# Token choice by one-hot matmuls: the one-hot tile and its values laid out with the contracted columns innermost

## The reference, cut to what matters

```
logits = x @ gate_w.T                      # 4096 tokens x 16 experts
scores = softmax(logits, axis=-1)
for each expert e: the 512 tokens with the highest score[:, e] are chosen
out   += score * (gelu(x Wg) * (x Wu)) Wd  # of the chosen tokens alone
out   += shared expert of all tokens
```

## Time and profile before

| what | us |
|---|---|
| median of three runs | 4539.38 |
| profiled execution, its own time | 4539.38 |
| span of its trace | 4537.7 |
| TensorE matmul busy | 3656.6 (81%) |
| VectorE busy | 2486.8 (55%) |
| ScalarE busy | 1439.2 (32%) |
| GpSimd busy | 1668.4 (37%) |
| from the first `hot` comparison to the copy of `slots` | 3699.21 to 3761.30 |

### The profile page before, as it was taken

One profiled execution on the slowest core, in us unless ns is written; L12 is line 12 of the kernel. 1 busy time (PEld: TensorE's weight loads), 2 busy tenths in 40 slices (PEclk: granted clock), 3 DMA queues, 4 the chain that ended last, 5 costly groups with the idle time before them and its releaser, 6 DMA issues. The chain is left out here.

```text
span 4537.7 us, 53885 instructions
## 1 busy us (share of the span) xinstructions
PE 3656.6 (81%) x17474; PEld 1672.2 (37%) x17563; DVE 2486.8 (55%) x3976; ACT 1439.2 (32%) x2018; POOL 1668.4 (37%) x1362
## 2 busy tenths in 40 slices
PE   8889999979997899977596504057797998999994
PEld 3322222223332433325354302023355554555553
DVE  5589999945552155533523497955695572111113
ACT  2247777743332233332132302011253221111111
POOL 0032222226665056662263073723552221222221
PEclk9979999989998999988698756578898998999997
DMA  5542323211102511113224402023354013333333
GB/s 174 186 74 60 73 62 69 56 58 35 38 26 73 193 37 38 40 41 116 91 85 137 168 17 93 0 84 92 114 155 151 28 38 109 105 97 92 103 82 83
DMA packets 323883, 382.97 MB, mean 84 GB/s; under 512 B 52016, under 2 KB 252992, under 8 KB 322688
## 3 DMA queue, kind: packets, MB, share of 16 engines
q1 hardware_dynamic: 270912, 285.83, 20.4%
q0 software_dynamic: 35776, 73.97, 6.4%
q10 hardware_dynamic: 17024, 20.97, 1.3%
HBM read 240.69 MB, written 135.76 MB: 83 GB/s over the span
## 5 line engine op out<-in xcount | busy, mean ns | idle before, releaser
L571 DVE TENSOR_REDUCE modulated_mx<-modulated_ring 128x1 f32<-128x512 f32 x1024 | 651.5, 683 | 52.2 <-PE modulated_ring L478 46.0
L555 ACT ACTIVATE modulated_probs<-modulated_scores 128x1024 f32<-128x1024 f32 x512 | 496.1, 1021 | 182.0 <-PE modulated_scores L499 181.9
L2861 DVE TENSOR_TENSOR expert_h<-expert_gelu,expert_bank 128x512 f32<-128x512 f32 x128 | 88.0, 688 | 391.6 <-PE expert_bank L2829 391.6
L2789 POOL DMA_INDIRECT scratch_acc<-expert_y,expert_idx x64 | 101.0, 1579 | 485.0 <-DVE expert_y L2866 442.9
L508 PE MATMUL modulated_acc<-modulated_probs,modulated_v 128*32 128x512 f32 x2048 | 273.5, 606 | 0.6 <-ACT modulated_probs L555 0.6
L478 PE MATMUL modulated_ring<-modulated_k,modulated_q 64*128 64x512 bf16 x1024 | 239.5, 399 | 34.1 <-DMA modulated_v<-scratch_v 23.0
L499 PE MATMUL modulated_scores<-modulated_q,modulated_k 128*128 128x512 bf16 x945 | 255.7, 383 | 10.9 <-issue 5.1
L910 POOL TENSOR_TENSOR causal_total<-causal_total,causal_probs 128x1024 f32<-128x1024 f32 x96 | 225.6, 2350 | 86.5 <-ACT causal_probs L831 85.5
L910 POOL TENSOR_TENSOR meta_total<-meta_total,meta_probs 128x1024 f32<-128x1024 f32 x96 | 225.6, 2350 | 86.5 <-ACT meta_probs L831 85.5
L2829 PE MATMUL expert_bank<-expert_xT,expert_wg 128*128 128x512 f32 x512 | 243.2, 598 | 7.8 <-ACT expert_xT L2841 7.8
L853 DVE TENSOR_REDUCE causal_mx<-causal_maxima 128x2 f32<-128x1024 f32 x120 | 146.0, 1217 | 183.8 <-PE causal_maxima L737 183.8
(11 more groups left out here) (471 smaller groups left out, 6970.1 us busy)
## 6 DMA issues: line engine op xcount, KB each, us to landing
expert_wg<-x_WgT SPq DMA_DIRECT2D x16, 1024.0 KB, 4.9
expert_wu<-x_WuT SPq DMA_DIRECT2D x16, 1024.0 KB, 6.9
expert_wd<-x_WdT SPq DMA_DIRECT2D x16, 1024.0 KB, 5.4
modulated_k<-scratch_k_part SPq DMA_DIRECT2D x192, 64.0 KB, 3.0
modulated_q<-scratch_q_part SPq DMA_DIRECT2D x192, 64.0 KB, 3.1
scratch_v<-proj_v SPq DMA_DIRECT2D x8, 1024.0 KB, 6.7
modulated_v<-scratch_v SPq DMA_DIRECT2D x16, 512.0 KB, 4.6
scratch_M<-steps_snap SPq DMA_DIRECT2D x16, 512.0 KB, 3.3
```

The source lines that it names most:

```text
L555: nc.scalar.activation(probs[u % NPROBS][i][:], sc[i][:], ACT.Exp, scale=SCALE).then_inc(s_exp, 1)
L571: V.tensor_reduce(mx[h % 2][:, x // 2, 1 - j % 2, j // 2, x % 2:x % 2 + 1], ring[bank_of["max", 4 * m + j]][:], AX.X, ALU.max).then_inc(s_ ...
L2789: added[j].done(G.indirect_dma_start(out=scr["acc"], out_offset=bass.IndirectOffsetOnAxis(ap=idx[j][a][:], axis=0), in_=y[j][:, a, :], in_ ...
```

## The change: layout of the one-hot tile and of the values

The shapes are turned round; the computation and the results are the same.

```
-        B_ = st.sb("values", [P, CT * VALS, NT, NE], BF16)
+        B_ = st.sb("values", [P, NT, NE, CT * VALS], BF16)
...
-        cols, low = st.sb("cols", [P, P, NE], BF16), full("low", BF16)
-        hot = [st.sb(f"hot{j}", [P, P, NE], BF16) for j in range(2)]
+        cols = st.sb("cols", [P, P])
+        hot = [st.sb(f"hot{j}", [P, NE, P], BF16) for j in range(2)]
...
-            G.iota(cols[:], pattern=[[1, P], [0, NE]], ...)
+            G.iota(cols[:], pattern=[[1, P]], ...)
...
-  last = nc.tensor.matmul(slots[:, e, :], hot[t % 2][:, :, e], B_[:, :, t, e], ...)
+  last = nc.tensor.matmul(slots[:, e, :], hot[t % 2][:, e, :], B_[:, t, e, :], ...)
...
-            step(V.tensor_single_scalar(low[:], lo[:], 1.0, ALU.subtract))
+            step(V.tensor_single_scalar(lo[:], lo[:], 1.0, ALU.subtract))
...
-                step(tt(B_[:, a * VALS], where[a][:], tile_no[:], ALU.mult))
-                step(V.tensor_scalar(B_[:, a * VALS + 1], where[a][:], tok_no[:], None, ALU.mult))
+                step(tt(B_[:, :, :, a * VALS], where[a][:], tile_no[:], ALU.mult))
+                step(V.tensor_scalar(B_[:, :, :, a * VALS + 1], where[a][:], tok_no[:], None, ALU.mult))
                 for c in range(3):
-                    step(tt(B_[:, a * VALS + 2 + c], where[a][:], part[c][:], ALU.mult))
+                    step(tt(B_[:, :, :, a * VALS + 2 + c], where[a][:], part[c][:], ALU.mult))
...
-                tt(hot[t % 2][:], cols[:], low[:, t:t + 1, :].broadcast_to([P, P, NE]), ALU.is_equal).then_inc(s_hot, 1)
+                tt(hot[t % 2][:], cols[:].unsqueeze(1).broadcast_to([P, NE, P]), lo[:, t, :].unsqueeze(2).broadcast_to([P, NE, P]),
+                   ALU.is_equal).then_inc(s_hot, 1)
```

More of the change, by code:

```diff
@@ L2521, in _ @@
             G.affine_select(out=below[:], in_=below[:], compare_op=ALU.is_gt, fill=0.0, base=0, pattern=[[1, P]], channel_multiplier=-1).then_inc(s_made, 1)
-            G.iota(cols[:], pattern=[[1, P], [0, NE]], base=0, channel_multiplier=0, allow_small_or_imprecise_dtypes=True).then_inc(s_made, 1)
+            G.iota(cols[:], pattern=[[1, P]], base=0, channel_multiplier=0, allow_small_or_imprecise_dtypes=True).then_inc(s_made, 1)
             G.iota(tile_no[:], pattern=[[1, NT], [0, NE]], base=0, channel_multiplier=0, allow_small_or_imprecise_dtypes=True).then_inc(s_made, 1)
@@ L2612, in _ @@
                 for e in range(NE):
-                    last = nc.tensor.matmul(slots[:, e, :], hot[t % 2][:, :, e], B_[:, :, t, e], start=(t == 0 and e == 0), stop=(t == NT - 1),
+                    last = nc.tensor.matmul(slots[:, e, :], hot[t % 2][:, e, :], B_[:, t, e, :], start=(t == 0 and e == 0), stop=(t == NT - 1),
                                             skip_group_check=True)
```

## The result

The changed kernel has a median of 4597.33 us over five runs (4588.27 to 4600.99), the kernel before one of 4542.89 over five: a ratio of 1.0122, 95% interval 1.0106 to 1.0138. That is 54 us slower. The forecast was 4562.5, with a range up to 4574: the sign was right, the size wrong, and the measured time lies outside the range.

A forecast was written before the change was run, and what follows sets the result against it. TensorE bounds the stretch up to tile 23, then both engines alternate; after the change VectorE does. Values 3.5, GpSimd 1.3 and 8.7, comparisons 70.5 and last tile 1.28 us give +23.2, forecast 4562.5 us, range 4549 to 4574.

The forecast's parts named there:

- the price of the values' writing: Ahead of the first comparison: products with `part` at 692 ns, `tok_no` ones at 426, 3.5 us more in all.
- the sum: Values' extra 3.5 us, GpSimd's 1.3 and 8.7, comparisons 70.5, last tile 1.28: copy of `slots` 23.2 us later.
- The comparison: The 32 one-hot comparisons on VectorE: starts 2.20 us apart instead of 1.14, 70.5 us of work against 36.6.
- GpSimd beside VectorE: GpSimd's `h` and `y` hold up a gapless VectorE: 1.3 us ahead of the comparisons, 8.7 beside them.
- my bound of 0.2 us: TensorE's loads and matmuls: only the last tile's 1.28 us counts, left as it is; bound 0 to -0.2.
- the first rival: TensorE's clock falls in the first part, a pair takes 6.1 us: 13 us more, 4576; chance 0.08.
- GpSimd does not cut in: Rival: comparisons hold their place and GpSimd waits, contention falls to today's or less: +13 to +17, 4554; chance 0.12.
- not slower: Rival: the comparison keeps more of its pace, under 1.90 us between starts TensorE hides it for 24 tiles; 4537; chance 0.06.

The follow-up runs named there:

- The added products: Kernel before, with 512-element products of various output and input steps added at the stage's end: bfloat16 outputs 730, 1295, 2424 ns at 4, 8, 16 bytes.
- the one-hot tile alone: Kernel before, with only the lines of `cols`, `low` and `hot` changed to the new layout: 4562.75 us, ratio 1.0046.

## Why the prediction was wrong

One row of the kernel before bears on the step that failed, a copy by ScalarE in another stage (min/median/max ns):

```profile
L1838 ACT ACTIVATE mproj_laid<-mproj_bank x16: 1005/1044/1073, 2577.9 to 2805.6; 128x512 f32<-128x512 f32 x16
```

- *The step that failed* is the price of the values' writing: "With an output that steps over 20 elements I take 692: 12 x 0.266 = 3.2 us; the bounds are 0 and 3.2", with "The products with `tile_no` stay" and an upper bound of 692 for `tok_no`. I looked for what a step does to the pace of the inputs (packed or not) and closed the range there, at the price of a dense output. The text says itself that "no row shows a stepped output alone"; the bound from above was then no bound. And one row did show it. ScalarE writes L1838 in the kernel before to every 16th float32 element and takes 1044 ns for 512, where its dense copies of 512 take 597 (L2554). That row, shown above, gives no 2399 ns, but it shows that a stepped output has a price of its own. Measured: 2399 ns for all sixteen two-input products and 1370 for the four others, and the stretch at 49.0 us against the 20.4 of the sum (15.6 + 3.5 + 1.3). The comparisons' stretch came out 2.3 us under the sum (78.2 against 80.5), so the two stretches missed by 26.3. The medians missed by 31.2 (54.4 against 23.2); the other 4.9 lie outside the stretches or in the spread between executions. The Trainium skill has the line that I did not weigh: "Advanced Engine Details and Errata", section "SBUF Cachelines", has lines of 16 bytes and a penalty where every access goes to another line. The added products agree with the 16 bytes, and in two-input products half-written words cost more than twice as much as the line alone.
- *The comparison* was right: 2279 ns, starts 2.20 us apart, from the nearest row by shape and repetition. That the one-hot tile alone landed on 4562.75 is in part chance, as said with that run.
- *GpSimd beside VectorE* was right in kind. Beside the comparisons it was 6.5 us (32 times 2481 less 2279, mean and median), not 8.7: all four `y` of the chunk before fell into the longer writing of the values, none on the comparisons. In the values' stretch I had added 1.3 us; it fell instead, from 3.9 to some 2.7.
- *TensorE* gained more than my bound of 0.2 us: the stage's end after the last comparison is 0.7 us, not 1.28. What I drew from the Trainium skill's "TensorE: Matmul & The Clock Gate", section "Weight-path perf modes — Fast Weight Load (FWL) and DoubleRow" (no gain from packed weights) goes further than the section does: it names packed and strided reads for the fast load, and that both are equally fast was my inference. The rows show otherwise: in the median, packed weights take 96 to 113 ns a load here, strided ones 167 to 168.
- *The clock* fell as the first rival says, to a mean of 0.77 in the first part, where I had said that under 0.9 would prove me wrong. It cost next to nothing: VectorE waited 0.3 us in all. A job at half speed takes 3.76 us, but two tiles only some 1.1, a pair 4.9 us, about what VectorE needs with GpSimd's share (4.4 and up to 1.3), and some jobs ran at full speed. The rival's price had all jobs at half speed and used the old 2.33.
- *GpSimd does not cut in* and *not slower* are out: 3.06 us for an `h` shows it waiting for a comparison, and then the next comparison waiting for it; and the comparisons start 2.20 us apart, above the 1.90 from which they decide.

## What to carry to other kernels

Price a new access pattern by its output as well as its inputs, and where no row shows a stepped output, leave the range open above: in a two-input product a lone 2-byte element every 16 bytes or more costs 4.4 ns, against 0.5 for an element of the dense comparison. A layout that helps the reader can be had for little if the writer's innermost index is a pair of neighbours in every tensor, all of them bfloat16. And with one engine made faster, look at once at how many buffers let it use that.

## What the runs showed of the hardware

- In a two-input product on VectorE, a bfloat16 output element that fills half of a 4-byte word costs 4.4 ns for each 16 bytes entered, a whole word some 1.8 ns. With one input VectorE pays half (1286 and 1346 ns for 512 elements with a step of 20, 2397 with two), and a memset nothing that shows (485 ns). ScalarE's copy takes 2441 ns with that step, 630 dense.
- A comparison with a repeated input keeps 1218 ns for 2048 elements if the repetition lies outside a pair of neighbours, and takes 2284 if the single element repeats (all tensors bfloat16).
- 16 weight loads and matmuls of 20 columns take 1.08 us with weights 32 bytes apart and values 1024 apart, 1.05 with neighbouring values alone, 0.67 with neighbouring weights alone, and 0.56 with both.
